# A decoder layer on one core: row sums of the last attention chunk, router logits, VectorE order and the last expert's rows

## What is computed

```
x = layernorm(x + self_attention(x))             # 16 heads of 32
x = layernorm(x + cross_attention(ctx, x))       # 8 heads of 64, 77 keys
logits = x_flat @ router_w.T                     # 8 experts, one is chosen per token
kept = pos < C                                   # C = 768 places per expert
h = gelu(einsum('ecd,edf->ecf', buf, w1) + b1)   # 512 -> 2048
eo = einsum('ecf,efd->ecd', h, w2) + b2
x = layernorm(x + eo[chosen_e, pos_c] * chosen_p * kept)
```

## Time and profile before

| | |
|---|---|
| median of 3 runs | 3720.26 us (3717.48 to 3720.76) |
| the profiled execution | 3720.95 us, with a span of 3719.2 us from the first to the last instruction |
| self-attention, cross-attention, experts | to about 2204, 2764 and 3719 us of the span |
| TensorE busy | 3454.1 us (93%) |
| VectorE, GpSimd, ScalarE busy | 67%, 55%, 45% |
| TensorE's granted clock, mean | 0.958 of full speed |

### The profile page before, as it was taken

The page is one execution under the profiler, slowest core; times in us unless marked ns, Lnnn a source line. Parts: engine busy times, 40 slices in busy tenths (PEclk is TensorE's granted clock), DMA queues, the critical chain, the costliest instruction groups (busy, mean ns, idle before and its releaser), DMA issues. The chain is left out here.

```text
span 3719.2 us, 50285 instructions
## 1 busy us (share of the span) xinstructions
PE 3454.1 (93%) x18109; PEld 2267.8 (61%) x18109; DVE 2508.9 (67%) x4510; ACT 1671.8 (45%) x3035; POOL 2053.2 (55%) x1025
## 2 busy tenths in 40 slices
PE   7999999999999999999999857999959999999996
PEld 5455455455455454554554325878849889988885
DVE  5777777777777777777777525778744665556667
ACT  2555555555555555555555533334312333223333
POOL 2689888888888888898888860011120011101111
PEclk9999999999999999999999878999969999999998
DMA  6321321312213122223210022122132243223333
GB/s 219 101 58 61 91 66 61 95 49 80 87 49 100 56 66 86 63 72 91 66 43 22 4 90 65 57 93 71 69 122 68 95 135 117 98 84 120 126 114 108
DMA packets 190274, 308.44 MB, mean 83 GB/s; under 512 B 25513, under 2 KB 72233, under 8 KB 190010
## 3 DMA queue, kind: packets, MB, share of 16 engines
q1 hardware_dynamic: 164330, 238.58, 20.6%
q0 software_dynamic: 14592, 44.32, 3.4%
q10 hardware_dynamic: 11088, 22.02, 1.7%
HBM read 195.66 MB, written 61.33 MB: 69 GB/s over the span
## 5 line engine op out<-in xcount | busy, mean ns | idle before, releaser
L463 DVE TENSOR_REDUCE sa_part_max<-sa_mx 128x1 f32<-128x512 f32 x2048 | 1281.6, 679 | 543.0 <-PE sa_mx L574 539.0
L426 ACT ACTIVATE sa_prob<-sa_sc 128x512 f32<-128x512 f32 x2048 | 1121.9, 595 | 823.3 <-PE sa_sc L620 780.5
L247 POOL TENSOR_TENSOR sa_quad_sum<-sa_quad_sum,sa_prob 128x1024 f32<-128x1024 f32 x512 | 1207.3, 2404 | 7.7 <-ACT sa_prob L426 7.7
L574 PE MATMUL sa_mx<-sa_k_stack,sa_q_stack 96*128 96x512 f32 x2048 | 967.0, 474 | 27.1 <-DVE sa_part_max L463 15.9
L620 PE MATMUL sa_sc<-sa_q_stack,sa_k_stack 98*128 98x512 f32 x2048 | 864.9, 424 | 8.2 <-ACT sa_prob L426 8.1
L247 POOL TENSOR_TENSOR sa_quad_sum<-sa_prob 128x1024 f32<-128x1024 f32 x256 | 616.3, 2431 | 257.5 <-ACT sa_prob L426 257.5
L574 PEld LDWEIGHTS sa_mx<-sa_k_stack,sa_q_stack 96*128 96x128 f32 x2048 | 389.5, 190 | 376.8 <-issue 205.5
L620 PEld LDWEIGHTS sa_sc<-sa_q_stack,sa_k_stack 98*128 98x128 f32 x2048 | 389.2, 190 | 318.7 <-ACT sa_prob L426 274.0
L1858 PE MATMUL ex_h<-ex_xT,ex_w 128*128 128x384 f32 (+2 forms) x2688 | 465.7, 329 | 41.6 <-issue 18.0
L589 PE MATMUL sa_pv<-sa_prob,sa_v 128*32 128x512 f32 x4096 | 502.8, 609 | 0.7 <-ACT sa_prob L426 0.7
L1858 PEld LDWEIGHTS ex_h<-ex_xT,ex_w 128*128 128x128 f32 x2688 | 447.7, 195 | 53.5 <-issue 25.4
(11 more groups left out here) (199 smaller groups left out, 3186.4 us busy)
## 6 DMA issues: line engine op xcount, KB each, us to landing
ex_w_in<-in_L_ffn_w_dram SPq DMA_DIRECT2D x130, 512.0 KB, 4.4
sa_xT<-xT SPq DMA_DIRECT2D x57, 1024.0 KB, 5.1
sa_q_stack<-sa_hilo SPq DMA_DIRECT2D x372, 64.0 KB, 2.0
sa_k_stack<-sa_hilo SPq DMA_DIRECT2D x360, 64.0 KB, 2.0
rows<-sa_empty SPq DMA_DIRECT2D x48, 257.0 KB, 3.8
ex_rows<-rows POOLq DMA_DIRECT2D x8, 1542.0 KB, 7.4
ex_xg<-rows POOLq DMA_DIRECT2D x48, 256.0 KB, 3.0
sa_prob<-in_x_dram ACTq DMA_DIRECT2D x8, 1024.0 KB, 6.9
```

The source lines that it names most:

```text
L247: pool.tensor_tensor(quad_sum[:, i % 2, heads, :], so_far, prob[:, k, heads, :], ALU.add).then_inc(quad_ready, 1)
L426: act.activation(prob[:, kt % 4, j, :], sc[n % 2][:, :], ACT.Exp, scale=SCALE).then_inc(prob_ready, 1)
L463: dve.reduce_max(part_max[:, q, j, k:k + 1], mx[n % 3][:, :], AX_X).then_inc(max_read, 1)
L574: pe.matmul(mx[n % 3][:, :], q_stack[0:QK, j, at:at + P], k_stack[0:QK, g // NQ % 2, j, k * BANK:(k + 1) * BANK], start=True, stop=True).t ...
```

## The change

**Last attention chunk.** GpSimd adds only the first quad. From step 4 on TensorE sums the probabilities themselves (`last_sums`) in `last_burst`, which replaces `burst` from step 4 on; the first quad's `row_sums` moves to the burst of step 10. Five banks (`sc` and the three `mx`) hold scores. ScalarE no longer waits for GpSimd from step 8 on.

**Cross-attention.** `route_logits` takes the router as the weight (8 columns) and moves `x2T` (512 columns) into bank 6, ScalarE copies the 8 x 512 result (`leave_logits`, between the copies of probability tiles 1 and 2), and TensorE transposes it into bank 7 (`transpose_logits`, behind the transposes of probability tile 3). VectorE's order becomes: `low_p` 0 and 1, `norm1`, `residual2` 0, `low_p` 2, `place_tokens`, `low_p` 3, `residual2` 1, `choose`, `leave_x1nT`, `residual2` 2, `add_bias`, `residual2` 3, `variances`.

**Last expert.** In its steps (3, 1), (3, 2) and (3, 3) VectorE makes bias times gate plus residual for two tiles each (`first_sum`). Behind the products it adds the scaled accumulator in one instruction per tile, in two groups of three tiles, and GpSimd makes the power and the scatter by group. TensorE takes the last second layer's tiles in reverse and signals each. (Of the two functions `last_rows` below the first is GpSimd's and the second VectorE's.)

```diff
-            for g in range(CHUNKS):
+            for g in range(LAST):
...
-            divide(CHUNKS - 1)
+            for k in range(1, 4):
+                add_step(LAST, 0, k)
+            divide(LAST - 1)
+            divide(LAST)
...
-                        if j % 2 == 0 and step >= 4:
+                        if j % 2 == 0 and 4 <= step < LAST * T + 8:
...
+            def last_sums(kt, end):
+                for j in range(HG):
+                    last = pe.matmul(den[D * j:D * (j + 1), :], ones[:, :], prob[:, kt % 4, j, :],
+                                     start=(kt == 4), stop=(kt == T - 1))
+                if end:
+                    last.then_inc(den_mm, QUADS - 1)
+
+            def last_burst(kt):
+                if kt == 6:
+                    pe.wait_ge(dens_ready, LAST)
+                pe.wait_ge(prob_ready, (LAST * T + kt) * HG)
+                if kt == LAST_DEN_AT:
+                    row_sums(LAST * QUADS)
+                for step in (kt - 2, kt - 1):
+                    if step >= 4:
+                        last_sums(step, step == T - 1)
+                    add_values(LAST * T + step)
...
-                after(pe, prob_ready, n - 1)
+                after(pe, prob_ready, n - 4 if n >= LAST * T * HG + len(last_sc) else n - 1)
...
-            pe.wait_ge(prob_ready, CHUNKS * T * HG)
-            add_values(CHUNKS * T - 2)
-            add_values(CHUNKS * T - 1)
-            row_sums(CHUNKS * QUADS - 1)
+            last_burst(T)
...
                 if more:
                     norm1(n + 1)
+                residual2(n, (0,))
+                low_p(n, 2)
                 if n >= 2:
                     place_tokens(n - 2)
-                if n + 2 < NCH:
-                    add_bias(n + 2)
-                residual2(n, (0,))
-                low_p(n, 2)
+                low_p(n, 3)
                 residual2(n, (1,))
-                low_p(n, 3)
                 if n > 0:
                     choose(n - 1)
                 if more:
                     leave_x1nT(n + 1)
                 if n == PER_B - 1:
                     low_qk()
-                residual2(n, (2, 3))
+                residual2(n, (2,))
+                if n + 2 < NCH:
+                    add_bias(n + 2)
+                residual2(n, (3,))
                 variances(n, 1)
...
+            def leave_logits(n):
+                act.wait_ge(lg_mm, n * LG_MM + 1)
+                act.activation(lgT[:, :], bank[6][0:E, :], ACT.Copy).then_inc(x2T_ready, 1)
...
             def route_logits(n):
-                pe.wait_ge(x2T_ready, (n + 1) * KC)
+                pe.wait_ge(x2T_ready, n * LEFT + KC)
+                for k in range(KC):
+                    last = pe.matmul(bank[6][0:E, :], rw[:, k, :], x2T[:, k, :], start=(k == 0), stop=(k == KC - 1))
+                last.then_inc(lg_mm, 1)
+
+            def transpose_logits(n):
+                pe.wait_ge(x2T_ready, (n + 1) * LEFT)
...
                 for t in range(TQ):
-                    for k in range(KC):
-                        last = pe.matmul(bank[7][:, t * E:(t + 1) * E], x2T[:, k, t * P:(t + 1) * P], rw[:, k, :], start=(k == 0), stop=(k == KC - 1))
+                    last = pe.transpose(bank[7][:, t * E:(t + 1) * E], lgT[:, t * P:(t + 1) * P], ident[0:E, 0:E])
                 last.then_inc(lg_mm, 1)
...
+    FIRST_AT = {(3, 1): (5, 4), (3, 2): (3, 2), (3, 3): (1, 0)}
+    GROUPS = ((5, 4, 3), (2, 1, 0))
...
+            def last_rows():
+                e = E - 1
+                for i, group in enumerate(GROUPS):
+                    rows_of = slice(group[-1], group[0] + 1)
+                    pool.wait_ge(ve_ready, e + i + 1)
+                    pool.tensor_tensor(rstd[:, rows_of], var_eps[:, rows_of], minus_half[:, rows_of], ALU.pow).then_inc(rstd_ready, 1)
+                    for k, t in enumerate(group):
+                        pool.wait_ge(y_ready, e * TS + i * len(group) + k + 1)
+                        send_tile(t)
...
+            def first_sum(t):
+                if t == FIRST_AT[3, 1][0]:
+                    dve.wait_ge(in_b2, E * 16)
+                    dve.wait_ge(in_rows, E * 16)
+                    dve.wait_ge(scattered, (E - 1) * TS * 16)
+                dve.scalar_tensor_tensor(out=out[:, t, :], in0=b2[:, :], scalar=rows[:, t, C:C + 1],
+                                         in1=rows[:, t, 0:C], op0=ALU.mult, op1=ALU.add).then_inc(out_ready, 1)
+
+            def last_rows():
+                e = E - 1
+                for i, group in enumerate(GROUPS):
+                    for k, t in enumerate(group):
+                        done = i * len(group) + k
+                        dve.wait_ge(o_mm, E * STEPS - 1 + FREE + done + 1)
+                        dve.wait_ge(out_ready, (e + 1) * TS)
+                        dve.scalar_tensor_tensor(out=out[:, t, :], in0=acc[t][:, :], scalar=rows[:, t, C:C + 1],
+                                                 in1=out[:, t, :], op0=ALU.mult, op1=ALU.add).then_inc(sum_ready, 1)
+                        measure(e * TS + done, t)
+                    rows_of = slice(group[-1], group[0] + 1)
+                    dve.wait_ge(mv_ready, e * TS + (i + 1) * len(group))
+                    dve.tensor_scalar(var_eps[:, rows_of], mv[:, rows_of, 1], EPS, None, ALU.add).then_inc(ve_ready, 1)
+                for i, group in enumerate(GROUPS):
+                    dve.wait_ge(rstd_ready, e + i + 1)
+                    for t in group:
+                        dve.tensor_scalar(out[:, t, :], out[:, t, :], mv[:, t, 0:1], rstd[:, t:t + 1], ALU.subtract, ALU.mult).then_inc(y_ready, 1)
...
                     if e > 0 and (q, j) in SCALE_AT:
                         for t in SCALE_AT[q, j]:
                             scale_rows(e - 1, t)
+                    if e == E - 1 and (q, j) in FIRST_AT:
+                        for t in FIRST_AT[q, j]:
+                            first_sum(t)
```

More of the change, by code:

```diff
@@ L205, in after, with score_bank @@
                 engine.wait_ge(sem, value)
+        def score_bank(n):
+            first = LAST * T * HG
+            return sc[n % 2] if n < first else last_sc[(n - first) % len(last_sc)]
         def stacked_first(engine, what, n):
@@ L665, in _ @@
                         if i == 1 and kt % 2 == 0:
-                            burst(g, kt)
+                            if g == LAST and kt > 2:
+                                last_burst(kt)
+                            else:
+                                burst(g, kt)
                         if i == 2 and kt == T - EARLY and g + 1 < CHUNKS:
@@ L1368, in _ @@
                     leave_p(n, t)
+                    if n > 0 and t == 1:
+                        leave_logits(n - 1)
                 if more:
@@ L1685, in rstds, with send_tile @@
                 pool.tensor_tensor(rstd[:, :], var_eps[:, :], minus_half[:, :], ALU.pow).then_inc(rstd_ready, 1)
+            def send_tile(t):
+                pool.indirect_dma_start(out_rows, bass.IndirectOffsetOnAxis(ap=rows[:, t, C + 1:W].bitcast(I32), axis=0),
+                                        out[:, t, :], None, bounds_check=z.TOK - 1, oob_is_err=False).then_inc(scattered, 16)
             def send_rows(e):
@@ L1820, in _ @@
                     dve.tensor_tensor(out[:, t, :], acc[t][:, :], b2[:, :], ALU.add).then_inc(out_ready, 1)
-            for t in range(TS):
-                add_rows(E - 1, t)
-            add_eps(E - 1)
-            for t in range(TS):
-                scale_rows(E - 1, t)
+            last_rows()
         @block.tensor
@@ L1871, in second_layer, with last_layer @@
                 last.then_inc(o_mm, 1)
+            def last_layer(tiles):
+                step = E * STEPS - 1
+                pe.wait_ge(w2_ready, step + 1 + FREE)
+                pe.wait_ge(hT_ready, 2 * step + 2 + 2 * FREE)
+                if tiles < TS:
+                    pe.sem_inc(o_mm, TS - tiles)
+                for t in reversed(range(tiles)):
+                    for part, (ph, pw) in enumerate(PARTS):
+                        last = pe.matmul(acc[t][:, :], hT[:, 1, ph, t * P:(t + 1) * P], w2[:, 1, pw, :],
+                                         start=False, stop=(part == 2))
+                    last.then_inc(o_mm, 1)
             def next_rows(e, i, row):
@@ L1892, in expert @@
                         next_rows(e, i, 2 * q - 2 + j // 2)
-                second_layer(e, STEPS - 1, tiles)
+                if e + 1 < E:
+                    second_layer(e, STEPS - 1, tiles)
+                else:
+                    last_layer(tiles)
             def fewest(count, e, variants):
```

38 lines of the change are left out of this document (25 added, 13 removed).

## The result

Before 3720.51 us, after **3685.81 us** (medians of four runs each); ratio 0.9910, 95% interval 0.9897 to 0.9922, so some 35 us less where 18 were forecast. The profiled execution of the changed kernel took 3682.34 us, span 3680.5, mean granted clock 0.967 (before 0.958).

What follows compares the result with a forecast made beforehand. Neither TensorE nor GpSimd simply bound the last attention chunk; TensorE bound the cross-attention, a VectorE chain the last expert's end. From the profiled 3720.95: +0 - 27 + 8 = 3702 us, range 3688 to 3718.

Steps and rivals of the forecast that it cites:

- The tail (-3.8): End of the last attention chunk: 8.4 us from last exponential to last sums become 4.6 us, so -3.8 us.
- The longer bursts less the sums of quads (9.0 - 1.9 = +7.1): Last attention chunk: five bursts (6 to 14) get 9.0 us longer; sums of quads leave bursts 6 and 14, -1.9.
- Scores made ahead let six bursts start up to 0.25 earlier: -1.5: Last attention chunk: scores made ahead start six bursts up to 0.25 us earlier, estimated as half a pair's spacing; -1.5 us.
- Clock: -2: Last attention chunk: denser bursts should end the time at clock 0.50 sooner, -2 us, between -6 and +2.
- all of it: Cross-attention: the forecast's far end, -38 us, against -27 taken and -8 for only half of the waits.
- Over the passes I leave 8 of the 24.6 us: Cross-attention, VectorE's order: of 24.6 us that transposes wait for `low_p`, 8 stay, so -16 us.
- the +1.5 for the last logits: Cross-attention, last chunk: logits stand alone at half clock (7.00 us); copy, transposes and two handovers follow, +1.5 us.
- I take 17 of them back: Cross-attention clock: work at half speed costs 13 to 28 us, partly by logits, partly by stalls; 17 us won back.
- The price of the logits: Cross-attention: eight f32 products of 512 columns follow each other at 0.43 us, 3.4 us against 3.49 before.
- B: Rival, last expert: its rows are no hindrance, so -1 us instead of +8, 3693 us in all; chance 0.10.
- C: Rival, cross-attention: logits with eight columns of weights don't hold the clock, half the waits stay; -11, 3718 us; chance 0.14.
- D: Rival, cross-attention: `residual2` 0 waits for a late store, so `low_p` stays late; slower, about 3730 us; chance 0.06.

## Why the prediction was wrong

Too little by 16 us (3702 against 3685.81): about 5 in the last attention chunk, 6 in the cross-attention and 4 in the last expert by the timed runs of the parts, and 1 that lies within their intervals.

**Last attention chunk: forecast 0, measured -5 (-1 to -9), -8 by the stage.** The tail (-3.8) was right: from the end of the last exponential to the end of both copies it takes 4.8 us, before 9.1. The longer bursts less the sums of quads (9.0 - 1.9 = +7.1) were near: from the burst of step 6 to the last one it is +5.0, and +11.4 with two banks, where more of it is at the lower clock. The step that failed is "Scores made ahead let six bursts start up to 0.25 earlier: -1.5", together with "Clock: -2". I priced the banks by the handover of one pair, and only up to the next burst. In the runs they are worth 8.3 us in the six steps ahead of the first sums alone, and 17 us over the whole chunk beside the sums: ScalarE's eight exponentials shrink by 0.6 us, and the time at the lower clock falls from 42 to 17 us. How much of the 17 is the spacing and how much the clock was not separated.

**Cross-attention: forecast -27, measured -33 (-28 to -38), -37 by the stage.** The end "all of it" (-38) was nearer than the value taken. Both causes are in the runs, the logits and the stalls, and they act at separate places, so terms that add were right. But two steps were mis-sized. One is "Over the passes I leave 8 of the 24.6 us": 3.3 stayed, so -21.3 instead of -16. The other is the +1.5 for the last logits: 7.00 us before, they take 6.8 with the copy and the transposes (2693.71 to 2700.55). The clock's "I take 17 of them back" was near as a total, though it was a choice between 13 and 28 and so in part luck: TensorE's busy time fell by 16.3 us although the transposes came in (seven passes of 0.41, so 2.9 instead of 2.4). But only a part of it belongs to the logits, under which it stood. Alone they give -4, the order -25, where the terms gave -13 and -14. The price of the logits held: 3.60 us for eight products (3.4).

**Last expert: forecast +8, +7.6 to +8.3 by the stretch, +4 (+1 to +7) by the timed runs.** Each step is in the trace: the wait, the half-speed products behind it, the second power behind three scatters. The difference to the timed value lies in the noise of the rest of the stage, or was not resolved.

**The rivals.** B's "-1 instead of +8" is what the kernel with its own buffers showed (-2 against the old end), but the changed kernel does not do that. C's reason is out: the clock is 1.00 behind the new logits. D is out: the store has landed to within 1.3 us.

## What to carry to other kernels

Where the clock falls at several places, look at each by itself: what runs slower there, and what stood or ran just before. Here the slow products behind the logits and those behind the stalls were two places with two causes, and a wait cost its own length besides. To remove a stall, go on until nothing stands ahead of the input: moving one operation only moved the stall to the next tile, 25.8 us as before. More banks are not priced by one handover, since both engines go faster in every step up to the next thing that holds them. And before an operation is moved ahead, look at what its input's load waits for: the early sums stood behind the scatters of another expert, and a second buffer turned +8 us into -2.

## What was not expected of the hardware

- Eight exponentials of 128x512 took 4.65 us when the scores came by turns into two banks, and 4.02 when they lay ready.
- With the old logits of eight moving columns and no wait for the low parts over 1.4 us, the granted clock still fell directly behind them in passes 1, 3, 5 and 6 (`outputs` 0 5.3 us), and in passes 2 and 4 it did not (3.7 us). Behind the new ones `outputs` 0 took 3.7 to 3.8 us in each pass. The last expert's products behind a stall of 10.2 us took 4.16 us, before 2.27.
- With the same code the self-attention stage came out within 2.3 us in six profiled executions (2204.6 to 2206.9), the experts' stage, half as long, within 8 us in nine (947.7 to 955.9).
